# Projection weights stored as even and odd column halves, read by the matmuls in turns from both

## The reference, cut to what matters

```python
xn = _layernorm(x, norm_scale, norm_bias)
q = xn @ Wq + bq
k = xn @ Wk + bk
v = xn @ Wv + bv
...                                   # mask k and v, split into heads
q = softmax(q, axis=-1)
k = softmax(k, axis=2)
attn = einsum('bhse,bhsd->bhed', k, v)
y = einsum('bhtd,bhed->bhte', q, attn)
scale, shift = split(silu(emb) @ film_emb_W + film_emb_b, 2, axis=-1)
h = _layernorm(y, film_norm_scale, film_norm_bias) * (1.0 + scale) + shift
return x + silu(h) @ film_out_W + film_out_b
```

## Time and profile before

| What | Value |
|---|---|
| Median of the runs | 915.3 us |
| Profiled execution, its own time | 911.22 us |
| Its span | 908.9 us |
| Mean granted TensorE clock | 0.998 |
| TensorE matmul busy | 885.0 us, 97% of the span |
| VectorE, ScalarE, GpSimd busy | 613.2, 398.4, 285.5 us |
| DMA, mean rate | 86 GB/s |

### The profile page before, as it was taken

One profiled execution on the slowest core, in us unless ns is written; L12 is line 12 of the kernel. 1 busy time (PEld: TensorE's weight loads), 2 busy tenths in 40 slices (PEclk: granted clock), 3 DMA queues, 4 the chain that ended last, 5 costly groups with the idle time before them and its releaser, 6 DMA issues.

```text
span 908.9 us, 15990 instructions
## 1 busy us (share of the span) xinstructions
PE 885.0 (97%) x5883; PEld 736.4 (81%) x5883; DVE 613.2 (67%) x1317; ACT 398.4 (44%) x607; POOL 285.5 (31%) x323
## 2 busy tenths in 40 slices
PE   5999999999999999999999999999999999999998
PEld 4668788887888878788888888888888888888876
DVE  5668676875678677677795775656756575576754
ACT  6226335533444534344553543524345443444433
POOL 2013432404343131433314342132423214243520
PEclk9999999999999999999999999999999999999999
DMA  9672232132312203240130402103030020301202
GB/s 275 234 263 94 64 122 70 34 128 69 138 46 101 107 23 138 69 155 31 65 140 1 151 1 79 60 0 138 0 138 0 20 119 0 138 0 50 90 1 93
DMA packets 30556, 78.31 MB, mean 86 GB/s; under 512 B 11320, under 2 KB 11320, under 8 KB 24640
## 3 DMA queue, kind: packets, MB, share of 16 engines
q1 hardware_dynamic: 30528, 77.93, 23.4%
HBM read 61.12 MB, written 16.80 MB: 86 GB/s over the span
## 4 chain that ended last, share of the span: by engine, by line
PE 91%; DVE 4%; DMA 2%; issue 2%; ACT 1%; POOL 0%; SPq 0%; DVEq 0%; POOLq 0%; ACTq 0%
PE psum_w L419 54%; PE psum_k L419 20%; PE psum_k L659 5%; PE psum_k L626 3%; PE psum_t L649 3%; PE psum_t L492 3%; PE psum_t L479 2%; DMA x_mean_and_rstd<-x_mean_rstd 1%; DVE y L1050 1%; PE psum_t L444 1%; DMA x_in<-in_x 1%; DMA gate<-x_mean_and_rstd 1%; DVE x_in L733 0%; DVE q_rsum L1048 0%; DVE k_exp L965 0%
## 5 line engine op out<-in xcount | busy, mean ns | idle before, releaser
L1253 POOL TENSOR_TENSOR xT_low<-xT,xT_high 128x512 fp32r<-128x512 f32 x60 | 78.4, 1307 | 189.0 <-ACT xT_high L1126 187.7
L976 DVE TENSOR_TENSOR q<-psum_w,bias_q 128x512 f32<-128x512 f32 x64 | 44.3, 692 | 98.7 <-PE psum_w L419 98.7
L419 PE MATMUL psum_k<-w_high_k,xT_high 128*128 128x512 f32 x256 | 104.4, 408 | 4.0 <-DVE y L1050 2.0
L1157 ACT ACTIVATE gate<-psum_t,film_shift,film_scale 128x512 f32<-128x512 f32 x60 | 46.6, 776 | 138.8 <-PE psum_t L492 109.1
L419 PE MATMUL psum_w<-w_high_v,xT_high 128*128 128x512 f32 x256 | 101.3, 396 | 0.0
L419 PE MATMUL psum_k<-w_high_k,xT_low 128*128 128x512 f32 x256 | 100.9, 394 | 0.0
L419 PE MATMUL psum_k<-w_low_k,xT_high 128*128 128x512 f32 x256 | 100.6, 393 | 0.0
L419 PE MATMUL psum_w<-w_high_q,xT_high 128*128 128x512 f32 x256 | 100.1, 391 | 0.0
L419 PE MATMUL psum_w<-w_high_v,xT_low 128*128 128x512 f32 x256 | 99.7, 389 | 0.0
L419 PE MATMUL psum_w<-w_low_v,xT_high 128*128 128x512 f32 x256 | 99.7, 389 | 0.0
L419 PE MATMUL psum_w<-w_high_q,xT_low 128*128 128x512 f32 x256 | 99.6, 389 | 0.0
(11 more groups left out here) (148 smaller groups left out, 1828.6 us busy)
## 6 DMA issues: line engine op xcount, KB each, us to landing
x_in<-x_between_layers SPq DMA_DIRECT2D x9, 1024.0 KB, 4.7
x_res<-in_x SPq DMA_DIRECT2D x8, 1024.0 KB, 6.8
x_between_layers<-x_res SPq DMA_DIRECT2D x8, 1024.0 KB, 3.8
x_in<-in_x SPq DMA_DIRECT2D x7, 1024.0 KB, 4.8
x_res<-x_between_layers SPq DMA_DIRECT2D x7, 1024.0 KB, 6.7
out_x<-x_res SPq DMA_DIRECT2D x7, 1024.0 KB, 3.8
x_in<-in_x_turned SPq DMA_DIRECT2D x6, 1024.0 KB, 5.4
raw_weights<-in_L_cond_film_emb_W SPq DMA_DIRECT2D x4, 1024.0 KB, 7.1
```

The source lines that it names most:

```text
L419: mm = pe.matmul(bank, lhs[:, c, rows_of_tile], rhs[w][:, c, :], start=(c == 0 and n == 0), stop=(c == CHUNKS - 1 and n == 2))
L976: dve.tensor_tensor(q[:, t, :], psum_w[:, t % 2, :], bias_q[:, :], ALU.add)\
L1157: act.activation(gate[:, c % 2, :], psum_t[:, c % 2, :, :].rearrange("p t s -> p (t s)"), ACT.Silu, scale=film_scale[:, cond, c:c + 1].rea ...
L1253: pool.tensor_tensor(xT_low[:, c, :], xT[:, c % 2, :], xT_high[:, c, :], ALU.subtract)\
```

## The change

The host reorders the columns of the eight projection matrices: columns 0, 2, 4, ... come first, in positions 0 to 255 of each row, and columns 1, 3, 5, ... follow in positions 256 to 511. The matmuls of line 419 read the moving operand through a view that takes position 0, then 256, then 1, then 257, and so on. The stationary operand, the output in PSUM, the number of columns, the loads and the splits are as before.

```diff
@@ -152,6 +152,11 @@
+        def alternating(w):
+
+
+            return w.rearrange("p (a b) -> p b a", a=2)
+
@@ -416,7 +421,7 @@
                         for n, (lhs, rhs) in enumerate(((high, w_high), (high, w_low), (low, w_high))):
-                            mm = pe.matmul(bank, lhs[:, c, rows_of_tile], rhs[w][:, c, :],
+                            mm = pe.matmul(bank, lhs[:, c, rows_of_tile], alternating(rhs[w][:, c, :]),
                                            start=(c == 0 and n == 0), stop=(c == CHUNKS - 1 and n == 2))
@@ -1335,6 +1340,7 @@
+SPLIT_NAMES = [("L0_cond_", "L1_cond_")[layer] + name for layer in range(LAYERS) for name in NAMES[layer].values()]
@@ -1355,6 +1361,8 @@
     for name, value in inputs.items():
+        if name in SPLIT_NAMES:
+            value = np.asarray(value).reshape(DIM, DIM // 2, 2).transpose(0, 2, 1).reshape(DIM, DIM)
```

## The result

The changed kernel is faster: 888.66 us median of four runs (886.24 to 891.15) against 913.5 us for the kernel before, ratio 0.973 with an interval of 0.968 to 0.978. The forecast was 1565 us, with a range that began at 908. The profiled execution has a span of 888.9 us.

The account below looks back on a forecast made before the run. The prediction took TensorE's stream of columns to bound the kernel. To 911.2 us it added 3072 matmuls x 213 ns = 654 us, giving 1565 us, own range 1530 to 1620, 8-in-10 range 908 to 1850.

Parts of the forecast that it names:

- the one term of the sum: Line 419's moving operand read with neighbours 1024 bytes apart: 213 ns more on each of 3072 matmuls, 654 us.
- lower bound: Bound on the price of line 419's alternating read: nothing, with a gain excluded.
- The unit: Operand fetch at line 419 delivers one column per two clocks, 213 ns more per matmul; chance 0.38.
- VectorE's rows at line 847 and 828: VectorE's strided reads as bounds for line 419: 0.59 ns per element gives 1845 us, 0.13 gives 1120 us.
- nothing happens: Rival at line 419's moving read: fetch keeps up, matmuls stay at 227 ns, time 911 to 916 us; chance 0.26.
- The chance left for a gain: Whole kernel faster by some accident of timing, by over 1%; chance 0.02.
- The count of 3072: Number of matmuls at line 419, at 0.227 us each 697 us of the profiled execution.
- the 97.4 us foretold: Length of one iteration of the changed kernel: 56.5 us plus 192 matmuls at 0.213 us more.
- There is no cover over it: TensorE's column stream bounds the kernel, so any extra cost per column is paid 3072 x 512 times.

Follow-up runs that it names:

- halves: Matmul stream in a TensorE-only program without the computation, moving operand read through the change's view: 216 ns per fp32r matmul, against 227 for a plain run.
- e1: Changed kernel with the alternating view and host's order in layer 1 alone, layer 0 reading plain runs: 894.26 us, ratio 0.979.
- m2: Second TensorE-only program of 48-matmul streams, computation left out, with further walks of the moving operand: every second column of one run took 453 ns.
- m1: First TensorE-only program, computation left out: 20 streams of 48 matmuls, each with another view, type or stationary block; fp32r plain 227 ns.
- e8: Changed kernel with every x turned on TensorE, none by the host, and mean and rstd rows no longer sent through memory: 877.27 us, ratio 0.963.
- e11: e8 with only the store of mean and rstd rows put back, in 4-byte pieces, in iterations 1 to 6 of layer 0: 884.69 us, ratio 0.970.

## Why the prediction was wrong

**The step that failed** is the one term of the sum, 213 ns more per matmul for neighbours that lie apart; 11 ns less was measured. Its lower bound had shut out that sign: "A gain is excluded, since the stream runs at one column per clock already." The stream ran at one column per clock and 14 ns more, and the prediction had measured those 14 ns and then treated them as fixed. Eleven of them were the price of a plain fp32r read. Nothing in the trace said which part of a repeated cost is a floor; the plain bf16 stream and halves, both at 216 ns, do.

**The unit was wrong with it.** One column per two clocks was priced from line 444 for an operand whose neighbours lie in different lines. The row was misread besides: its 64 records belong to 32 matmuls, two each, so a float32 matmul takes four passes of its 512 columns and not two (859 ns in the plain float32 stream), and the 204 ns between two records are not one more pass of a matmul. Neighbours are the wrong thing to look at: 461 ns exists, but it takes a walk in which each of the two readers meets a new line each time. The view of the change has every second column next to the last but one, and none of the walks tried in fp32r was faster. VectorE's rows at line 847 and 828 told nothing about TensorE's read: 0.59 and 0.13 ns per element against -0.02 measured.

**The rival "nothing happens"** had the mechanism nearly right, that four consecutive columns of a side come from the same 16 bytes, and was given 0.26. It forecast no change in time, where 216 ns was measured against 227. The chance left for a gain was 0.02 and was called an accident.

**What held:** no instruction was added anywhere, and the granted clock stayed at 1.00 but for two short falls behind stalled blocks. The loads of the stationary operand are at 189 ns in the median, in the v projection, against 188, and the plain float32 matmuls of line 444, now 449, are at 593 as in the earlier trace rows. The count of 3072 was right. One row was taken too long: the earlier trace rows call 56.50 us an iteration, but the next k projection starts at 452.10 us, so that iteration took 54.30, and the 97.4 us foretold for the changed one had 2.2 us too many.

**"There is no cover over it" was only half right.** It holds in layer 1 (18.3 us of 17 arrived, e1). In layer 0 a chain of two DMAs and VectorE, and with it the stalls of the small matmuls, lay just under TensorE's time, and the prediction asked what would cover a loss, never what would cap a gain. The earlier trace rows show TensorE's blocks bounding the iteration, and no row said by how little.

## What to carry to other kernels

In fp32r, lay out the moving operand so that columns n and n + 2 are neighbours in memory: interleave within groups of eight columns on the host and read them back through the view, for 5% of each 512-column matmul; leave float32 and bf16 plain, where the halves cost 26% and 124% more and nothing tried was faster. Before pricing a change of a stream, compare the stream's repeat time with the fastest of its size seen anywhere, for the difference is what a change can win. And where an engine is busy all the time, look for the chain that would be next before counting on the gain: here the way of the rows through memory, with the stalls beside it, kept 11 us of 36, and its store in 4-byte pieces costs 7 us even where nobody reads the result.

## What the runs showed of the hardware

- Reading every second column of one fp32r run (steps of 8 bytes) doubles a matmul, 453 ns against 227, though no column is more than 8 bytes from the last (m2).
- For bf16 the alternating halves cost 484 ns against 216 (m1).
- A DMA store in 1024 pieces of 4 bytes took 9.75 us for 4 KB in the changed kernel. Put into e8 by itself, it stalled TensorE by 0.5 to 2.1 us in each block of short matmuls, while the long ones after its issue kept their 216 ns (27 steps from 205.94 to 211.77 us in e11).
